# An unused 128-byte tile ahead of the experts' buffers in a fused decoder layer

## What is computed

```python
E, K = (12, 3)                      # 12 experts, each token goes to 3
B, S, H, I = (2, 512, 512, 1280)    # H = 512 wide, hidden width I = 1280
logits = jnp.einsum('bsh,he->bse', x, Wr) + br
top_vals, top_idx = jax.lax.top_k(jax.nn.softmax(logits, axis=-1), K)
for e in range(E):
    ...
    h = jax.nn.relu(jnp.einsum('bsh,hi->bsi', x, w1[e]) + b1[e])
    h = jnp.einsum('bsi,ih->bsh', h, w2[e]) + b2[e]
    out = out + mask[..., None].astype(x.dtype) * (w_e * h)
```

## The kernel before

| tile | start before | modulo 256 | start of change | modulo 256 |
|---|---|---|---|---|
| si, tick, turn, b1_now | 22912, 22944, 22976, 23008 | 128, 160, 192, 224 | 128 more each | 0, 32, 64, 96 |
| xf | 23072 | 32 | 23200 | 160 |
| xh | 25120 | 32 | 25248 | 160 |
| xl | 27168 | 32 | 27296 | 160 |
| h | 29216 | 32 | 29344 | 160 |
| hh | 34336 | 32 | 34464 | 160 |
| hl | 39456 | 32 | 39584 | 160 |
| y | 44576 | 32 | 44704 | 160 |
| xg, b2_sb, stage | 49088, 53216, 57312 | 192, 224, 224 | the same | |
| w_lo, w_hi | 65504, 147424 | 224, 224 | the same | |
| attention: wq_hi, wk_hi, wv_hi, wo_hi and their lows | | 128 | the same | |
| attention: xT_hi, xT_lo | 176640, 180736 | 0 | the same | |
| attention: oT_hi, oT_lo | 215456, 217504 | 160 | the same | |
| attention: xkT_hi, xkT_lo (blocks 360 bytes apart) | 184832, 186272 | 0, 160 | the same | |

## Time and profile before

### The profile page before, as it was taken

The page is one execution under the profiler, slowest core; times in us unless marked ns, Lnnn a source line. Parts: engine busy times, 40 slices in busy tenths (PEclk is TensorE's granted clock), DMA queues, the critical chain, the costliest instruction groups (busy, mean ns, idle before and its releaser), DMA issues.

```text
span 1494.1 us, 27777 instructions
## 1 busy us (share of the span) xinstructions
PE 1379.5 (92%) x7868; PEld 1135.9 (76%) x7869; DVE 819.8 (55%) x1197; ACT 698.1 (47%) x1878; POOL 842.6 (56%) x955
## 2 busy tenths in 40 slices
PE   5899998799986279999999999999999999999994
PEld 3777776577765268888888888888888888888883
DVE  6788887599997884745264444647444452000013
ACT  3657666244554234454444544445444454444530
POOL 0456445244653067767576676767766666565640
PEclk9999998899997589999999999999999999999985
DMA  7000000253333335545254344445444443151146
GB/s 268 1 1 0 0 0 26 82 188 97 111 99 136 153 115 126 147 113 137 66 148 105 106 106 111 124 113 156 107 111 95 123 112 77 35 154 35 31 132 232
DMA packets 77576, 152.42 MB, mean 102 GB/s; under 512 B 9120, under 2 KB 13728, under 8 KB 77024
## 3 DMA queue, kind: packets, MB, share of 16 engines
q1 hardware_dynamic: 62496, 115.09, 24.2%
q0 software_dynamic: 14320, 35.40, 12.0%
q10 hardware_dynamic: 720, 1.44, 0.3%
HBM read 119.31 MB, written 32.59 MB: 102 GB/s over the span
## 4 chain that ended last, share of the span: by engine, by line
PE 62%; DMA 2%; DVE 0%; SPq 0%; issue 0%; ACT 0%; DVEq 0%; POOL 0%; POOLq 0%
PE ps_h L1962 9%; PE ps_h L1967 9%; PE ps_h L1963 9%; PE ps_y L1985 9%; PE ps_y L1986 9%; PE ps_y L1989 9%; PE ps_td L1975 4%; PE ps_xd L1947 2%; DMA w_lo<-acc 1%; PE ps_xd L1996 0%; DMA xg<-xnd,gi 0%; DMA acc<-y,si 0%; DVE w_lo L1783 0%; SPq L1671 0%; DVE w_lo L1752 0%
## 5 line engine op out<-in xcount | busy, mean ns | idle before, releaser
L1962 PE MATMUL ps_h<-w_hi,xh 128*128 x708 | 251.5, 367 | 1.5 <-ACT xh L1878 1.4
L1963 PE MATMUL ps_h<-w_lo,xh 128*128 x708 | 244.3, 356 | 0.0
L1687 DVE TENSOR_TENSOR w_lo<-stage,w_hi 128x512 f32 x220 | 226.6, 1030 | 28.6 <-DVE w_hi L1685 2.9
L1985 PE MATMUL ps_y<-w_hi,hh 128*128 x590 | 238.8, 405 | 0.0
L1986 PE MATMUL ps_y<-w_lo,hh 128*128 x590 | 233.6, 396 | 0.0
L1820 POOL TENSOR_TENSOR y<-y,b_sb 128x512 f32<-128x512 f32 x58 | 79.7, 1374 | 226.6 <-ACT y L1903 226.6
L1810 POOL TENSOR_TENSOR hl<-h,hh 128x1280 fp32r<-128x1280 f32 x59 | 180.9, 3067 | 17.9 <-ACT hh L1897 17.5
L1903 ACT ACTIVATE y<-ps_y,wt 128x512 f32<-128x512 f32 x59 | 40.6, 688 | 293.5 <-PE ps_y L1989 293.5
L1884 ACT ACTIVATE h<-ps_h 128x512 f32<-128x512 f32 x177 | 80.7, 527 | 196.5 <-POOL hl L1810 185.6
L1967 PE MATMUL ps_h<-w_hi,xl 128*128 x708 | 166.7, 357 | 0.0
L1893 ACT ACTIVATE h<-ps_td,b_now 128x128 f32<-128x128 f32 x590 | 159.0, 392 | 3.9 <-PE ps_td L1975 1.2
(11 more groups left out here) (256 smaller groups left out, 2647.6 us busy)
## 6 DMA issues: line engine op xcount, KB each, us to landing
stage<-in_wcat SPq DMA_DIRECT2D x220, 256.0 KB, 3.0
front<-in_ctx_rev SPq DMA_DIRECT2D x32, 192.0 KB, 2.4
w_lo<-in_wcat SPq DMA_DIRECT2D x4, 1280.0 KB, 11.7
acc<-added_c POOLq DMA_DIRECT2D x1, 4352.0 KB, 17.4
front<-kpad SPq DMA_DIRECT2D x16, 256.0 KB, 3.4
toe<-kpad SPq DMA_DIRECT2D x16, 256.0 KB, 3.6
x2d<-xs SPq DMA_DIRECT2D x16, 256.0 KB, 2.4
xnd<-xn_c SPq DMA_DIRECT2D x16, 256.0 KB, 2.0
```

Of the source, the lines that this page charges most:

```text
L1687: nc.vector.tensor_tensor(lo, stage[:, c % NSTAGE], hi.bitcast(F32), ALU.subtract).then_inc(split_done, 1)
L1962: nc.tensor.matmul(out, x_hi, part(w_hi, e, k * FF + lo, hi - lo), start=(k == 0), stop=False)
L1963: nc.tensor.matmul(out, x_hi, part(w_lo, e, k * FF + lo, hi - lo), start=False, stop=False)
L1985: nc.tensor.matmul(ps_y[:], h_hi, part(w_hi, e, KD * FF + k * D, D), start=(k == 0), stop=False)
```

## The change

One tile, `lead`, of 128 partitions by 32 float32 values, is allocated first in the experts' stage. Nothing writes or reads it. All tiles that the stage allocates from the left start 128 bytes later: `xh`, `xl`, `hh` and `hl` go from 32 to 160 modulo 256. The weights stay at 224 modulo 256, so the stationary operands, which stood 64 bytes behind the weights' lines (32 - 224 + 256), stand 192 bytes behind them (160 - 224 + 256).

```diff
@@ -1558,6 +1558,8 @@
         def sem(name):
             return ctx.enter_context(nc.semaphore(name))
 
+
+        lead = sb("lead", [P, 32])
         si = sb("si", [P, 2], U32)
         tick = sb("tick", [P, 5])
         turn = sb("turn", [P, 1])
```

## The result

The changed kernel takes 1478.91 us (median of 4 runs, 1477.12 to 1481.78) against 1493.8 us before in the same comparison: a ratio of 0.9906, 95% interval 0.9885 to 0.9927. The profiled execution took 1480.42 us against 1495.83.

A forecast was written before the change was run, and what follows sets the result against it. The prediction took TensorE's own pace in the experts' stage as the bound. Its terms, all 0, left the profiled 1495.83 us at 1495.8 and the median at 1493.5 us, the forecast time, with a range of 1479 to 1508.

The forecast's parts named there:

- What bounds the kernel: Experts' stage: TensorE alone sets its length, busy in 930.21 of 930.50 us, 15.55 us a tile.
- the count: Experts' stage: 3186 matmuls of 512 columns, so one ns in each is 3.2 us.
- The step that failed: TensorE's 512-column matmuls: 233.3 ns kept at distance 192, change 0, with -4.1 to +3.8 us around it.
- The 256-column matmuls: First product's 708 matmuls on TensorE: change 0, with -2.3 us as an end if they take the shorter rhythm.
- The other engines: ScalarE and GpSimd, working on the moved tiles: change 0, a gain held impossible since TensorE doesn't wait for them.
- The transposes: TensorE's transposes in the experts' stage: given no term of their own in the prediction's sum.
- The slower rival: Experts' 512-column matmuls: more hold-ups at the new distance, 2.5 to 5 ns each, 1501.5 to 1509.5 us; chance 0.22.
- The faster rival: Experts' matmuls: fewer hold-ups at the new distance, 230 ns each, 1480.5 to 1483 us; chance 0.18.

The follow-up runs named there:

- e10: Changed kernel with an unused tile of 224 bytes, which puts the operands at distance 32; ratio 1.0002 to the kernel before.
- e6: Changed kernel with an unused tile of 64 bytes, which puts the operands at distance 128; ratio 0.9983 to the kernel before.
- e3: Against the kernel before, only xf, h and y moved to 160 modulo 256, stationary operands left at 32; 1494.23 us, ratio 0.9999.
- e12: Against the changed kernel, stationary operands cut from one tile at distance 176, xf, h and y at 32 modulo 256; ratio 0.9939 to the kernel before.
- e13: Changed kernel with one more tile ahead of h: first product at distance 192, second at 0; 1477.07 us, ratio 0.9878 to the kernel before.
- e5: Changed kernel with an unused tile of 32 bytes, which puts the operands at distance 96; ratio 1.0023 to the kernel before.
- e2: Against the kernel before, only xh, xl, hh and hl moved to 160 modulo 256, xf, h and y left at 32; 1477.12 us, ratio 0.9884.
- e4: Against the kernel before, weights moved 128 bytes lower, left-side tiles unmoved, so distance 192; 1477.15 us, ratio 0.9891.
- e1: Changed kernel with an unused tile of 256 bytes, which puts operands back at distance 64; 1494.38 us, ratio 0.9997 to the kernel before.
- e9: Changed kernel with an unused tile of 192 bytes, which puts the operands at distance 0; ratio 0.9888 to the kernel before.

## Why the prediction was wrong

**What bounds the kernel** was right: TensorE alone sets the experts' stage, busy in 930.21 of 930.50 us. So was the count: 3186 matmuls of 512 columns, 3.2 us for each ns. That its pace had something to give rests on the spacing at the lower clock. The windows view of the kernel before has a granted clock of 0.50 over the stretch of the earlier trace rows (columns as in the earlier trace rows):

```profile
266.27:268.83 2.56, 2.56 (x7) 1.98 (x6) 1.05 (x2) 0.00 (x0) 0.00 (x0) 0.50 0.00 0
```

The experts' own matmuls, at distance 64, show both clocks within one second product, at the end of the stage:

```profile
1453.72 0.63 PE L1986 MATMUL ps_y<-w_lo,hh 128*128 x1
...
1456.71 0.63 PE L1985 MATMUL ps_y<-w_hi,hh 128*128 x1
...
1457.77 0.39 PE L1986 MATMUL ps_y<-w_lo,hh 128*128 x1
...
1459.87 2.50 PE L1989 MATMUL ps_y<-w_hi,hl 128*128 x10
```

Seven take 2.99 us at 0.50, 427 ns each, and nine take 2.10 us at 1.00, 233.3 ns. Half of the 426.7 ns of the earlier trace rows is 213.3, so by this estimate each has about 20 ns over it at the higher clock. The convolution's float32 matmuls have hardly any: in the trace of the kernel before three of them take 1.44 us at 0.50 (starts 279.56 to 281.00), 480 ns each, and nine take 2.18 us at 1.00 (401.94 to 404.12), 242.2 ns, 2 ns over the half.

**The step that failed** is "I take for 192 the same 233.3 ns", and the reason given with it, that "this looks like a loss that is set by how much is read in parallel, and not by where it begins". The three distances read from the trace before, 32, 64 and 128, were read correctly: whole kernels at 32 and 128 came out within 0.2% of the kernel before (e10, e6). But they are three of six places on a plateau, and 192 isn't on it. Three nearly equal samples bound nothing between or beyond them when the course has narrow dips. That term is -12.4 us instead of 0 (1416 x -3.4 ns in the first product, 1770 x -4.3 ns in the second).

**The 256-column matmuls**, 0 with an end at -2.3 us, measured 708 x -4.2 ns = -3.0 us, so the end was too near as well. The two rhythms that the earlier trace rows show do exist, and the change leads into one as fast as the faster of them (113.3 against 114.2 ns).

**The other engines** at 0: right within the interval, by e3 (0.9999); its tiles are 0.026 us longer, 1.5 us in all.

**The transposes** have no term in the sum, which so takes 0 for them, and no row of before shows that they don't depend on the place. What the runs showed is 0: from the first transpose of `h` to the next product it is 994.36 - 993.35 = 1.01 us in the kernel before, 987.57 - 986.56 = 1.01 us in the changed kernel and 790.11 - 789.10 = 1.01 us in e3.

**The slower rival** read a pair of matmuls with 80 against 184 bytes and put 2.5 to 5 ns on the new distance. The sign was wrong: e12 at 176 and the changed kernel at 192, on either side of 184, were both faster than before. e13 shows that matmuls early in a run need not have the pace at which it settles, so that pairs in a changing distance tell little of a steady run.

**The faster rival** had the direction, a pace of 230 ns and 1480.5 us. The last two came within 1 ns and 2 us of what was measured (229 ns, 1478.91 us). That it came so near was luck: its 230 ns were read at distances 32, 136, 240 and 88 with 90 loaded columns, and whole kernels at or near three of these (32, 128, 96) lie within 0.25% of the kernel before (e10, e6, e5). It had 0.18; with an estimated 20 ns in each matmul that nothing else accounted for and a place never sampled, it deserved more.

What stays open is why 192 and 0 are faster, and how a product's rhythm carries over to the next. The runs show that the distance decides (e2 and e4 at 1477 us, e3 at 1494), that 256 bytes more change nothing at 64 (e1, 0.9997) and that a run of matmuls has a settled step (233.3 ns at 64, 226.7 at 0). No experiment took the load from beside a matmul or changed its length, so that the load holds the matmuls up was the author's guess and is not shown, and no rule follows that would have named 192 and 0 ahead of time.

## What to carry to other kernels

When TensorE bounds a kernel and is never idle, compare the distance between the starts of its matmuls with half of what it is at the lower clock. If it is clearly longer (here 233 ns at a clock of 1.00 against half of 427 at 0.50, for float32r matmuls with a load of 189 ns beside each), the mutual place of stationary and moving operand modulo 256 bytes is something to try that costs one unused tile and no instruction. Only this kernel shows a gain from it. Sweep it on the chip in steps of 32 bytes or less rather than argue from neighbours: here six of eight places gave the same within 0.4% and two gave 1%. And since any small tile that is added ahead of the operands moves them too, a change of 1% behind such an edit may be of this kind; padding to a full 256 bytes tells (e1).

## What was unexpected of the hardware

- A run of matmuls can need some ten matmuls to settle: 232 ns each at first, 226.7 ns after (e13). The same operands at the same addresses settle after two steps behind another first product (e9).
- The pace repeats to the nanosecond where all distances between the operands and the transposed tile `h` are the same: 15.547 us a tile in the kernel before and in e1, 15.287 in the changed kernel and in e4. With `h` at another place it differs a little at the same distance (15.573 in e3, 15.273 in e2).
- VectorE's subtraction of the weights' halves, whose operands weren't moved, went from a mean of 1030 ns to 975 in the changed kernel, while its rounding of `w_hi` from `stage` went from 575 ns to 654. With 220 of each, the two together rose from 353.1 to 358.2 us. TensorE never waited for them, so they have no part in the result, and the cause wasn't looked into.
